# One layer's attention issues its scores before half of its output, and its feed-forward pieces stand half a step earlier

## The reference, cut to what matters

```python
def _L3_xattn_ref(inputs_q, inputs_kv, Wq, Wk, Wv, Wo):
    q = (inputs_q @ Wq).reshape(b, sq, H, HD) * (1.0 / np.sqrt(HD))
    k = (inputs_kv @ Wk).reshape(b, skv, H, HD)
    v = (inputs_kv @ Wv).reshape(b, skv, H, HD)
    scores = jnp.einsum('bqhd,bkhd->bhqk', q, k)
    attn = jax.nn.softmax(scores, axis=-1)
    ctx = jnp.einsum('bhqk,bkhd->bqhd', attn, v).reshape(b, sq, H * HD)
    return ctx @ Wo

def _L3_ffn_ref(x, w_gate, w_up, w_down, up_reorder_index, down_reorder_index):
    ...
    qx, sx, sc = _reorder_quantize_x(xf, up_reorder_index)
    g = _qlinear(qx, sx, sc, w_gate, up_reorder_index, out_idx=down_reorder_index)
    u = _qlinear(qx, sx, sc, w_up, up_reorder_index, out_idx=down_reorder_index)
    t = jax.nn.silu(g) * u
    qt, st, sct = _reorder_quantize_x(t, down_reorder_index)
    y = _qlinear(qt, st, sct, w_down, down_reorder_index)

x = x + _L3_xattn_ref(_layernorm(x, axis=-1), ctx_2048, L3_xattn_Wq, ...)
x = x + _L3_ffn_ref(_layernorm(x, axis=-1), L3_ffn_w_gate, ...)
```

## Time and profile before

| | us |
|---|---|
| median of 3 runs | 1847.93 |
| lowest, highest | 1846.61, 1858.82 |
| the profiled execution, its own time | 1844.32 |
| its span in the trace | 1842.5 |
| mean granted TensorE clock in it | 0.941 |

### The profile page before, as it was taken

One profiled execution on the slowest core, in us unless ns is written; L12 is line 12 of the kernel. 1 busy time (PEld: TensorE's weight loads), 2 busy tenths in 40 slices (PEclk: granted clock), 3 DMA queues, 4 the chain that ended last, 5 costly groups with the idle time before them and its releaser, 6 DMA issues. The chain is left out here.

```text
span 1842.5 us, 29067 instructions
## 1 busy us (share of the span) xinstructions
PE 1555.6 (84%) x9134; PEld 1119.8 (61%) x9134; DVE 1333.8 (72%) x3791; ACT 821.8 (45%) x2363; POOL 638.0 (35%) x750
## 2 busy tenths in 40 slices
PE   4898889795557888888995999998978999889984
PEld 3443344463236677666774887887854555788873
DVE  6899797898868898989887356656564333478777
ACT  3133444573546776766773233332321221345552
POOL 1400021575647778878774201111120001221000
PEclk9899999898669999999998999999998999899996
DMA  4255300200929000000002400000262222522110
GB/s 160 69 148 173 130 1 1 86 2 7 209 104 364 22 1 1 1 2 1 1 1 80 139 1 28 13 12 12 89 192 67 87 87 77 197 91 105 62 40 12
DMA packets 103590, 132.48 MB, mean 72 GB/s; under 512 B 14160, under 2 KB 89136, under 8 KB 99472
## 3 DMA queue, kind: packets, MB, share of 16 engines
q1 hardware_dynamic: 94448, 112.39, 19.3%
q0 software_dynamic: 8992, 18.23, 4.0%
HBM read 85.75 MB, written 46.94 MB: 72 GB/s over the span
## 5 line engine op out<-in xcount | busy, mean ns | idle before, releaser
L2455 PE MATMUL l2fa_psQ<-l2fa_xT,l2f_home 128*128 128x128 f32 x1024 | 123.7, 280 | 6.3 <-DMA l2f_home<-in_L2f_kvT 6.3
L2455 PEld LDWEIGHTS l2fa_psQ<-l2fa_xT,l2f_home 128*128 128x128 f32 x1024 | 120.5, 196 | 8.6 <-DMA l2f_home<-in_L2f_kvT 6.7
L653 POOL TENSOR_TENSOR l0f_diag<-g_identb,l0f_mask 128x1024 bf16<-128x1024 bf16 x16 | 31.9, 2021 | 203.4 <-PE l0f_psA L948 191.6
L3235 POOL TENSOR_TENSOR route_rrms<-route_vrms,g_minus_half 128x1 f32<-128x1 f32 x8 | 5.6, 705 | 268.1 <-DVE route_vrms L3257 268.1
L2952 ACT ACTIVATE l2x_probs<-l2x_psS,l2x_nmax 128x128 f32<-128x128 f32 x256 | 90.9, 376 | 13.7 <-DVE l2x_nmax L2871 13.7
L3824 POOL DMA_INDIRECT routed_rows<-rows,route_slot_of x32 | 31.6, 986 | 181.6 <-DMA rows<-moe_yg 170.3
L2783 POOL TENSOR_TENSOR l2x_vsm<-l2x_vraw,l2x_smooth_row 128x512 f32<-128x512 f32 x64 | 91.8, 1435 | 0.0
L2774 POOL TENSOR_TENSOR l2x_probs<-l2x_probs,l2x_rtotal 128x512 f32<-128x512 f32 x64 | 66.6, 1041 | 69.6 <-DVE l2x_rtotal L2877 69.6
L3645 DVE COPY moe_xgT<-moe_psX 128x256 f32<-128x256 f32 x47 | 20.0, 425 | 91.6 <-PE moe_psX L3754 91.6
L3094 PEld LDWEIGHTS l2x_psS<-l2x_kT,l2x_qT 128*128 128x128 f32 x512 | 65.7, 191 | 23.4 <-issue 22.0
L1591 ACT ACTIVATE l2fa_probs<-l2fa_psS,l2fa_bias 128x128 f32<-128x128 f32 x128 | 45.3, 366 | 76.5 <-DVE l2fa_bias L1575 76.5
(11 more groups left out here) (545 smaller groups left out, 4641.8 us busy)
## 6 DMA issues: line engine op xcount, KB each, us to landing
rows<-g_row SPq DMA_DIRECT2D x1, 18304.0 KB, 60.1
kT_ctx<-l0f_held SPq DMA_DIRECT2D x32, 256.0 KB, 3.6
v_ctx<-l0f_held SPq DMA_DIRECT2D x32, 256.0 KB, 3.7
l3a_kT<-kT_ctx SPq DMA_DIRECT2D x8, 1024.0 KB, 5.1
l3a_v<-v_ctx SPq DMA_DIRECT2D x8, 1024.0 KB, 5.6
l0f_wrow<-in_L_ffn_w SPq DMA_DIRECT2D x24, 256.0 KB, 3.0
moe_xg<-rows SPq DMA_DIRECT2D x47, 128.0 KB, 2.0
rows<-moe_yg SPq DMA_DIRECT2D x47, 128.0 KB, 1.7
```

The source lines that it names most:

```text
L2455: last = nc.tensor.matmul(psQ[bank][:, j, :], w[:, c, h * HD:(h + 1) * HD], xT[u][:, c, :], start=(c == 0), stop=(c == KC - 1))
```

## The change

The lags of ten pieces become smaller by one, so that they are issued half a step earlier: `x_quantise` 2 to 1, `turn_x` and `copy_x` 4 to 3, `gate_and_up` 5 to 4, `take` 0 and 1 6 to 5, `take` 2 and `silus` 7 to 6, `turn_t` and `copy_t` 16 to 15, `down` 17 to 16, `finish` 19 to 18. `x_stats`, `hidden`, `level` and `snap` keep theirs. The tail loses takes 0 and 1 of batch 6, which the last quad now issues. On VectorE the even half of the side work is called between the maxima (and the add) and the copy of values, no longer after normalise. On TensorE the scores of quad n+1 come right after the projection, the output of quad n-1 is cut into two heads ahead of the odd half and two heads behind the turn. All of it holds for `causal` false; the `l2fa` stage keeps its order.

```diff
-        s = self.at_slot(h, 2)
+        s = self.at_slot(h, 1)
         if s is not None:
             self.x_quantise(dve, s)
...
-        s = self.at_slot(h, 6)
+        s = self.at_slot(h, 5)
         if s is not None:
             self.take(dve, s, 0)
             self.take(dve, s, 1)
...
     def end_vector(self, dve, G, added):
-        for k in range(self.TAKES):
-            self.take(dve, B - 2, k)
+        self.take(dve, B - 2, 2)
...
                 def quad(b, u, i, pieces, more, inputs):
+                    h = 2 * (QUADS * b + i)
                     at.maxima(nc, dve, QUADS * b + i, i % 2)
                     if i == 1 and not is_zero(b):
                         add(b - 1)
+                    if not causal:
+                        side.on_vector(dve, G, h, added)
                     if not (is_zero(b) and i == 0):
                         copy_values(*quad_before(b, u, i, QUADS))
...
                     at.normalise(nc, dve, QUADS * b + i, i % 2)
-                    side.on_vector(dve, G, 2 * (QUADS * b + i), added)
+                    if causal:
+                        side.on_vector(dve, G, h, added)
...
-                def output(b, u, i):
+                def output(b, u, i, heads):
 
                     n = QUADS * b + i
-                    pe.wait_ge(oT_ready, n + 1)
...
+                    if heads.start == 0:
+                        pe.wait_ge(oT_ready, n + 1)
...
+                        if i == 0:
+                            wait(pe, added, b)
+                    for j in heads:
...
-                    last.then_inc(oT_used, 1)
+                    if heads.stop == 4:
+                        last.then_inc(oT_used, 1)
+
+                OUTPUT_FIRST = range(0, 4) if causal else range(0, 2)
+                OUTPUT_REST = range(OUTPUT_FIRST.stop, 4)
...
                     for piece in pieces:
                         project(*piece)
+                    if more and not causal:
+                        scores(*quad_behind(b, u, i, QUADS))
                     if before:
-                        output(*before)
+                        output(*before, OUTPUT_FIRST)
                     side.on_tensor(pe, G, 2 * (QUADS * b + i) + 1)
                     if i == 2 and inputs:
                         prepare(b + 2, u)
                     at.turn(nc, pe, QUADS * b + i, i % 2, G.ident[:, :])
-                    if more:
+                    if more and causal:
                         scores(*quad_behind(b, u, i, QUADS))
+                    if before and OUTPUT_REST:
+                        output(*before, OUTPUT_REST)
```

More of the change, by code:

```diff
@@ L2052, in on_vector @@
             self.hidden(dve, s)
-        s = self.at_slot(h, 2)
+        s = self.at_slot(h, 1)
         if s is not None:
             self.x_quantise(dve, s)
-        s = self.at_slot(h, 19)
+        s = self.at_slot(h, 18)
         if s is not None:
@@ L2068, in on_vector @@
             self.take(dve, s, 1)
-        s = self.at_slot(h, 7)
+        s = self.at_slot(h, 6)
         if s is not None:
@@ L2105, in on_scalar @@
     def on_scalar(self, act, h):
-        s = self.at_slot(h, 4)
+        s = self.at_slot(h, 3)
         if s is not None:
             self.copy_x(act, s)
-        s = self.at_slot(h, 7)
+        s = self.at_slot(h, 6)
         if s is not None:
             self.silus(act, s)
-        s = self.at_slot(h, 16)
+        s = self.at_slot(h, 15)
         if s is not None:
@@ L2167, in on_tensor @@
     def on_tensor(self, pe, G, h):
+        s = self.at_slot(h, 15)
+        if s is not None:
+            self.turn_t(pe, G, s)
         s = self.at_slot(h, 16)
         if s is not None:
-            self.turn_t(pe, G, s)
-        s = self.at_slot(h, 17)
-        if s is not None:
             self.down(pe, s)
-        s = self.at_slot(h, 4)
+        s = self.at_slot(h, 3)
         if s is not None:
             self.turn_x(pe, G, s)
-        s = self.at_slot(h, 5)
+        s = self.at_slot(h, 4)
         if s is not None:
@@ L2481, in values @@
                     at.values(nc, pe, QUADS * b + i, v[u], i, oT_ready, QUADS * b + i)
-                def output(b, u, i):
+                def output(b, u, i, heads):
                     n = QUADS * b + i
-                    pe.wait_ge(oT_ready, n + 1)
[L2487 to L2491, removed]
+                    if heads.start == 0:
+                        pe.wait_ge(oT_ready, n + 1)
+                        if is_zero(b) and i == 0:
+                            pe.wait_ge(wo_loaded, 16)
+                        if i == 0:
+                            wait(pe, added, b)
+                    for j in heads:
                         last = nc.tensor.matmul(psY[:, :], oT[:, i % 2, j, :], wo[:, 4 * i + j, :],
                                                 start=(i == 0 and j == 0), stop=(i == QUADS - 1 and j == 3))
-                    last.then_inc(oT_used, 1)
+                    if heads.stop == 4:
+                        last.then_inc(oT_used, 1)
+                OUTPUT_FIRST = range(0, 4) if causal else range(0, 2)
+                OUTPUT_REST = range(OUTPUT_FIRST.stop, 4)
                 def quad(b, u, i, pieces, more, inputs):
@@ L2508, in quad @@
                     at.turn(nc, pe, QUADS * b + i, i % 2, G.ident[:, :])
-                    if more:
+                    if more and causal:
                         scores(*quad_behind(b, u, i, QUADS))
+                    if before and OUTPUT_REST:
+                        output(*before, OUTPUT_REST)
                 def finish():
                     values(B - 1, 1, QUADS - 1)
-                    output(B - 1, 1, QUADS - 1)
+                    output(B - 1, 1, QUADS - 1, range(0, 4))
                     side.end_tensor(pe, G)
```

## The result

The changed kernel takes 1837.72 us, the kernel before, beside it on the same chip, 1847.17 (medians of 17 runs each). The ratio is 0.9942, with a 95% interval from 0.9928 to 0.9956: faster by 0.6%, and inside the one per cent named in the prediction as no change. The measurement is finer than that: the interval is 0.3% wide and leaves out 1. The profiled execution has a span of 1837.6 us.

A forecast was written before the change was run, and what follows sets the result against it. Neither engine alone was the bound: VectorE's 25.65 us a batch plus waits set the period. Gains of 1.7 + 2.2 + 3.3 + 1.7 = 8.9 us led to 1839.0, given as 1838, range 1830 to 1850.

The forecast's parts named there:

- one per cent named in the prediction as no change: Whole kernel: 18.5 us is about what a measurement can tell from no change; chance of landing within it 0.94.
- Quad 0 to quad 1: From first reciprocal to second quad's in a batch: 5.95 us against 7.18 before, with VectorE waiting 1.5.
- Quad 1 to quad 2: Middle of a batch: maxima of quad 2 at 10.78 us, tokens transposed at 15.6, VectorE waiting 1.3 for them.
- Period: Middle batches: VectorE's own 25.65 us plus waits of 1.5 and 1.3 make 28.45, 1.1 less per batch.
- The change neither adds to it nor takes from it: Inside the batch loop: VectorE's own work stays 25.65 us a batch, so only the waits can change.
- The batches: Gain by batch: 0 for batches 0 and 1, then 1.7 us, two at 1.1, last three stretches 3.3.
- Tail: After the last add: takes 0 and 1 with their scale go, gaining 1.7 us.
- come out even: Last stretch: moved takes stand ahead of the last copy of values, offset by level moving ahead of the normalise.
- Every wait filled: Rival, whole stage: TensorE's 27.21 us becomes the period, 2.3 us gained per batch, time 1832; chance 0.13.
- Only the tail gains: Rival, batches and tail: waits move but still sum to 3.9 us, only 1.7 gained, time 1846; chance 0.14.
- The clock falls in the last batch: Rival, last batch: TensorE idles 2.9 us, then runs at half speed, costing 4 to 8.5 us, time 1844; chance 0.20.
- The tokens late: Slower rival, VectorE's copy of transposed tokens in quad 2: four batches lose 1.9 us each, time 1850.5; chance 0.05.

The follow-up runs named there:

- e4: Changed kernel with the input's rounding (x_quantise) put back from lag 1 to lag 2; ratio to the kernel before 0.9904.
- e5: Changed kernel with takes 0 and 1 of batch 6 put back in the tail; ratio to the kernel before 0.9947.
- e7: e4 with the whole output of the quad before ahead of the turn in quad 0 only; ratio to the kernel before 0.9914.
- e6: Changed kernel with the whole output of a quad ahead of the turn again, not halved; ratio to the kernel before 1.0046.
- e3: Kernel before with only VectorE's even side work moved ahead of the copy of values; median 1869.42 us, ratio 1.0115.
- e1: Kernel before with only the smaller lags and takes 0 and 1 out of the tail; median 1866.84 us, ratio 1.0085.
- e8: The same kernel as e4, measured once more; ratio to the kernel before 0.9920.

## Why the prediction was right

**Quad 0 to quad 1.** Forecast 5.95 (its terms add up to 5.93), measured 5.82. The turned copy, the two copies of tqT, the table load and the exponentials follow one another on ScalarE without a gap, as added up. The wait here was to be 1.5, of which up to 0.9 in the add; it is 0.8 in the add, 0.25 at the reciprocal and 0.2 at the copy, 1.2 to 1.3. The table switch has no drain beside it: the load starts at 1700.37, lasts 1.28, and the silu starts at 1701.66. What the Trainium skill prices for it, in "ScalarE: Activation LUTs", section "What ACT_TABLE_LOAD costs", would, as an estimate, have made this chain 1.4 us longer; the trace agrees with the bare load.

**Quad 1 to quad 2.** Forecast: maxima at 10.78, tokens at 15.6, a wait of 1.3. Measured: 10.64, 15.58, 1.5. This was the step with the widest unknown, and its middle held. e4 shows that its cause was named rightly, the rounding ahead of the maxima.

**Period.** 25.65 of VectorE's own work and 2.8 of waits, 28.45; measured 25.7 and 2.7, 28.44 and 28.50. "The change neither adds to it nor takes from it" holds.

**The batches.** Batches 0 and 1 were taken at 0: batch 1 is 26.04 against 25.97 (1614.03 to 1640.00), and batch 0 took 24.69 in e5, which has the same code there, against 24.61. The batch after them gained 1.47 (forecast 1.7), the next two 1.05 and 1.11 (2.2 together, as forecast), the last three stretches 1.85, 0.60 and 1.34, together 3.8 (3.3). That last sum came out by luck: the prediction had each of the three keep the shorter way from quad 0 to quad 1, and the last two do not. There that way was 7.91 and 7.19 us and is 7.93 and 7.06, as the turn starts 3.06 and 2.19 us after the reciprocal (1758.76 and 1785.28) in place of 0.95; from there on it is the 4.87 us of the middle batches. Their gain lies from quad 2 to quad 3, which went from 5.97 and 5.98 to 5.20.

**Tail.** 2.40 against 1.70. The takes were worth the 1.7 that the prediction gave them. The other 0.7 is TensorE's clock in that execution, which it did not count and which no run ties to the takes. Its remark that the moved takes come out even in the last batch is wrong by 0.5 us (e5).

The sum was 8.9; the trace gives 9.8, and the medians 9.4. The mechanism of the middle batches held; that the whole came this close owes something to the last stretches and to the clock of the tail.

**The rivals.** *Every wait filled* would have been 27.21 a period; e4 comes to 27.41 with one number put back, so that rival lay one step from the change. Its floor was not fixed: TensorE is busy for 26.71 us a batch in the changed kernel and 26.74 in e4. *Only the tail gains* is out, with 7.4 of 9.8 us gained ahead of it. *The clock falls in the last batch* did happen, but one quad earlier and cheaper than worked out. In the last batch the clock is 1.00 but for a stretch from about 1790 to 1794; windows of 2 us:

```profile
1788.00:1790.00 2.00, 0.52 (x4) 0.12 (x2) 1.79 (x5) 1.99 (x9) 0.72 (x1) 1.00 0.00 0
1790.00:1792.00 2.00, 1.74 (x9) 1.77 (x10) 1.79 (x4) 0.11 (x2) 0.00 (x0) 0.61 0.03 8
1792.00:1794.00 2.00, 2.00 (x8) 1.53 (x8) 1.86 (x6) 0.00 (x0) 0.00 (x0) 0.54 0.00 0
1794.00:1796.00 2.00, 2.00 (x16) 1.73 (x13) 1.90 (x6) 0.70 (x2) 0.00 (x0) 1.00 0.00 0
```

The timeline of TensorE there:

```profile
1790.26 1.88 PE L1607 MATMUL l3a_psS<-l3a_kT,l3a_qT 128*128 128x128 f32 x8 [1.74 <-ACT l3a_probs L1591]
1791.93 1.91 PE L2496 MATMUL l3a_psY<-l2f_home,l3a_oT 128*128 128x256 f32 x4
...
1797.53 1.13 PE L1607 MATMUL l3a_psS<-l3a_kT,l3a_qT 128*128 128x128 f32 x8 [1.35 <-ACT l3a_probs L1591]
```

After 1.74 us without work the scores take 1.88 in place of 1.13 and half an output 1.91 in place of 1.03, which is 1.6 us of TensorE's time; then the clock is back. The next scores come 7.38 us after the reciprocal of quad 1 (1790.15 to 1797.53), where the prediction had 7.3, and TensorE waited 1.35 us for them in place of the 2.9 that were worked out: the slow work lay in that gap and cost the chain nothing. The forecast price of 4 to 8.5 rested on a clock that falls in the gap and stays low to the last output. A dip of this kind stands in the last batch of every experiment but e7, and not in the kernel before. From quad 1 to quad 2 of that batch e4, with a dip, and e7, without, both take 7.07 us. *The tokens late*: they were 1.5 late, as the forecast had it. With 1.0 us more output ahead of each turn, in e6, they were 2.3 late, and with the two other waits a gain of 1.1 us a period became a loss of 0.9.

## What to carry to other kernels

When two engines each wait for the other, count what one of them does and each of its waits, and ask for every moved piece which wait it fills and which one it stands in front of. Three edits that by themselves cost 24, 19 and 2.5 us of the stage (by the medians 18, 21 and nothing) gained 10 together; judge such an order as a whole, and then put its numbers back one at a time, since one of them (here the rounding, 1.0 us a period) may be against the rest. In a tail with little work, read what a step is worth from several traces: here the clock of the engine behind it moved the tail by 0.3 to 0.8 us, with the step and without.

## What was not expected of the hardware

TensorE's clock does not answer to the length of one wait alone. A wait of 1.74 us in the last batch was followed by work at half speed; one of 2.43 us in the tail was followed by transposes at full speed (0.62 at 1820.26), and half speed came only with the next projection (1.57 at 1821.83). In the kernel before, waits of 2.93 and 2.89 us were followed once by full and once by half speed; and in the tails of e3 and e1 full speed followed a wait of 2.89 us and half speed one of 1.20. The Trainium skill, "TensorE: Matmul & The Clock Gate", section "HAM oscillation — how this bites in real kernels", has an array that was idle begin its next burst cold; the waits of 1.20 us in e1, of 1.74 us and of 2.89 us in the kernel before agree, those of 2.43 us, of 2.93 us and of 2.89 us in e3 do not.

In the profiled execution of the changed kernel the clock also fell in batch 0, where a projection took 3.58 us in place of the 1.95 of the earlier trace rows, and VectorE and ScalarE had to wait for it. The timeline, and the window of that projection (columns as above):

```profile
1595.84 3.58 PE L2458 MATMUL l3a_psQ<-l3a_xT,routed_wq 128*128 128x128 f32 x16
```

```profile
1595.84:1599.21 3.37, 3.37 (x19) 3.37 (x17) 1.47 (x3) 0.35 (x3) 2.03 (x2) 0.51 0.33 94
```

The quad from 1596.64 to 1604.41 was 7.77 us long. In e4, e5 and e8 the code is the same there, TensorE's two waits ahead of that projection are the same to 0.01 us (0.97 and 0.67), the clock of batch 0 is 1.00, and the quad took 6.14. So the same instructions after the same waits ran at either clock. That is 1.6 us of one execution and not of the change, and it hid a part of the gain: the span fell by 4.9 us only. Together with the start of the stage, which lay between 1586 and 1597 us in these traces though the edits leave the stages ahead of it as they were, it is a reason to set traces against each other by the stage and not by their spans.
